# Attention beside a mixture of experts on one core: unread products, a table of slot places with gathers, and sums copied within HBM

## The reference, cut to what matters

```python
xn = _layernorm(x, axis=-1)
x = x + _L0_attn_ref(xn, ...) + _L0_ffn_ref(xn, ...)

# attention, 64 pairs of sequence and head, 1024 x 1024 scores each
attn_weights = einsum('btd,bsd->bts', q, k) + _rel_to_abs(einsum('btd,md->btm', q, rel_k[0]))
attn_probs = softmax(attn_weights)
attn_output = einsum('bts,bsd->btd', attn_probs, v) + einsum('btm,md->btd', _abs_to_rel(attn_probs), rel_v[0])
return out @ Wo + bo

# experts
top_w, top_idx = top_k(softmax(x @ gate_w + gate_b), 2)       # weights normalised over the two
h = silu(einsum('td,edf->tef', x, w1)) * einsum('td,edf->tef', x, w3)     # 256 -> 1024
out = einsum('ted,te->td', einsum('tef,efd->ted', h, w2), combine)        # 1024 -> 256
```

## Time and profile before

| | |
|---|---|
| timed runs | 1829.11, 1821.48, 1824.39 us |
| median | 1824.39 us |
| the profiled execution | 1838.71 us |
| its span, first to last instruction | 1837.0 us |
| mean granted TensorE clock | 0.945 |
| busy: PE, PEld | 1694.4 (92%), 1022.4 (56%) |
| busy: DVE, ACT, POOL | 1437.7 (78%), 1099.4 (60%), 826.2 (45%) |
| DMA | 342.69 MB, mean 187 GB/s |
| L1193, VectorE's maxima | 512 of 1.22 us |
| L1506, accumulating scatters | 78 of 1.80 us |
| L1748, VectorE's weight splits | 304, mean 1.03 us |

### The profile page before, as it was taken

The page is one execution under the profiler, slowest core; times in us unless marked ns, Lnnn a source line. Parts: engine busy times, 40 slices in busy tenths (PEclk is TensorE's granted clock), DMA queues, the critical chain, the costliest instruction groups (busy, mean ns, idle before and its releaser), DMA issues. The chain is left out here.

```text
span 1837.0 us, 35484 instructions
## 1 busy us (share of the span) xinstructions
PE 1694.4 (92%) x13756; PEld 1022.4 (56%) x13756; DVE 1437.7 (78%) x2540; ACT 1099.4 (60%) x2133; POOL 826.2 (45%) x595
## 2 busy tenths in 40 slices
PE   5998799999999999999998999999999999999991
PEld 3774223333333333333334778888788888788880
DVE  3556979998887788878675998999989999987652
...
GB/s 166 349 334 278 62 18 147 164 100 150 169 160 159 154 166 161 139 156 145 36 118 145 225 227 237 239 245 248 222 238 230 250 245 237 220 211 193 210 121 189
DMA packets 195752, 342.69 MB, mean 187 GB/s; under 512 B 33392, under 2 KB 145920, under 8 KB 187392
## 3 DMA queue, kind: packets, MB, share of 16 engines
...
...
## 5 line engine op out<-in xcount | busy, mean ns | idle before, releaser
L1193 DVE CUSTOM_DVE_ANT_0 w2s<-t_s,hide 128x1024 bf16<-128x1024 f32 x512 | 607.2, 1221 | 129.6 <-PE t_s L1048 110.0
L1328 ACT ACTIVATE t_pr<-t_s 128x512 f32<-128x512 f32 x1024 | 559.4, 604 | 186.7 <-PE t_s L1062 132.8
L1048 PE MATMUL t_s<-ks,qs 48*128 48x512 f16 x1024 | 373.4, 419 | 41.6 <-DVE t_mx L1193 25.5
L1677 ACT ACTIVATE e_sg<-e_pa,down 128x256 f32<-128x256 f32 x312 | 147.7, 473 | 399.6 <-PE e_pa L1568 395.5
L1058 PE MATMUL t_s<-qs,ks 50*128 50x512 f16 x1024 | 366.0, 402 | 10.4 <-ACT t_pr L1328 7.9
L1075 PE MATMUL t_po<-t_pr,t_vx 128*32 128x256 f32 x4096 | 348.6, 413 | 0.5 <-issue 0.3
L1577 PE MATMUL e_py<-w2s,e_hT 128*128 128x256 f32 x1248 | 323.2, 382 | 0.0
L1748 DVE SCALAR_TENSOR_TENSOR ks<-big,up,qs 128x512 f16<-128x512 f32 x304 | 310.5, 1032 | 13.5
L1506 POOL DMA_INDIRECT expert_sums<-e_y,e_token x78 | 140.5, 1801 | 293.1 <-DMA expert_sums<-e_y,e_token 203.7
L1568 PE MATMUL e_pa<-xh,qs 128*128 128x256 f16 x1248 | 240.3, 274 | 20.7 <-DVE xl L1740 17.9
L1568 PE MATMUL e_pa<-xl,qs 128*128 128x256 f16 x1248 | 239.7, 274 | 0.0
...
## 6 DMA issues: line engine op xcount, KB each, us to landing
...
```

The source lines that it names most:

```text
L1048: last = nc.tensor.matmul(s1[:, buf, half * CH:(half + 1) * CH], qs[lows, u, h, i * P:(i + 1) * P], ks[lows, u, h, half * CH:(half + 1) * ...
L1193: nc.vector.tensor_tensor_reduce(out=seen[:, buf, :], in0=s1[:, buf, :], in1=c["hide"][:, (TB - 1 - row) * P:(TB - 1 - row) * P + L], scal ...
L1328: nc.scalar.activation(pr[:, k % BP, n % HG], s2[:, turn(u, n)], ACT.Exp, scale=SPREAD ** -2).then_inc(exp_ok, 1)
```

## The change

1. **Unread products.** `idle_turns(count)` on TensorE multiplies two constants (128 x 128 by 128 x 512, 16 bits) into PSUM buffers of pass 2, which nobody reads. 18 stand ahead of the first `pass1`, 3 behind every full tile up to `rows_first` (18 tiles), 28 at the place where VectorE chooses experts, and 3 after each of 3 further tiles.
2. **First maximum rows.** For the first half of the first group the four DMAs of the second part are issued by ScalarE instead of SyncE.
3. **A table of slot places.** `slot_rows` (1040 bytes per place) becomes `slot_table` with 16 bytes, the `meta` of the row. It is filled by two DMAs of 128 x 39 runs of 16 bytes each (the spare row numbers of 128 x 2 rows behind T) behind `step(0, ...)`, beside a store of 256 rows of zeros to the normed rows. `send` scatters only `meta` (the same 64 indirect scatters, of 128 x 16 bytes); the eight loads of 512 KB in `load_rows` go.
4. **The table comes back.** SyncE, at the place where it loaded the rows of slot 0, reads the table in two parts (8 and 31 slots: 2048 and 7936 runs of 16 bytes) into SBUF. GpSimd casts each part to row numbers; after the first it issues four indirect gathers of 128 normed rows each (slots 0 and 1). After the second it writes `ones`.
5. **Gathers in the expert stage.** The rows of slot s + 1 come by two gathers of GpSimd at the head of its slot s, ahead of `xb` and `prod`. The gates of all slots are computed once (`gates`, in slot 0); `rows_of` goes.
6. **Sums.** The two scatters of `put` no longer wait for each other, only for those of the slot before. The attention result of a tile is added to `expert_sums` by a third accumulating scatter (`add_rows`), which waits until the two have landed; `put` of the next slot waits for it. `res` keeps two tiles.
7. **The end.** `combine` goes. SyncE copies the sums to the output from HBM to HBM, 8 DMAs of 512 KB, inside the expert stage's block.

```diff
-        xn=dram("xn_rows", [T, E], F32),
+        xn=dram("xn_rows", [T + ST * P, E], F32),
-        xs=dram("slot_rows", [NS * TS, XE], F32),
-        moe=dram("expert_sums", [T + P, E], F32),
+        slots=dram("slot_table", [NS * TS, 4], F32),
+        moe=dram("expert_sums", [T + ST * P, E], F32),
...
+def gather_rows(nc, dr, xr, token, came, s, u):
+    for i in range(ST):
+        nc.gpsimd.indirect_dma_start(
+            out=xr[:, u, i, 0:E], out_offset=None, in_=dr["xn"],
+            in_offset=bass.IndirectOffsetOnAxis(ap=token[:, s * ST + i:s * ST + i + 1], axis=0)).then_inc(came[u], 16)
...
# attention, SyncE
+                            if half == 0 and j == 1:
+                                continue
                 step(0, 0, 2, 0)
                 sp.wait_ge(zero_ok, 2)
-                for z in range(N_ZERO // 2):
-                    sp.dma_start(zeros[z], zero[:].broadcast_to([P, 6, XE])).then_inc(zero_out, 16)
+                for i in range(ST):
+                    sp.dma_start(zeros[i], zero[:, i:i + 1, E:XE].broadcast_to([P, NS, XE - E])).then_inc(zero_out, 16)
+                sp.dma_start(dr["xn"][T:T + ST * P].rearrange("(i p) e -> p i e", p=P), zero[:, :, 0:E]).then_inc(zero_out, 16)
...
                 load_split(0, 1)
-                for u in range(2):
-                    sp.wait_ge(sent[u], 16 * NT)
-                sp.dma_start(xr[:, 0], slot_rows[0]).then_inc(x_in[0], 16)
+                sp.wait_ge(sent, 32 * NT)
+                slots_v = dr["slots"].rearrange("(n p) f -> p n f", p=P)
+                for i, part in enumerate((slice(0, CHUNK), slice(CHUNK, NS * ST))):
+                    sp.dma_start(tab[:, part], slots_v[:, part]).then_inc(tab_in[i], 16)
                 load_second(0)
-                sp.dma_start(xr[:, 1], slot_rows[1]).then_inc(x_in[1], 16)
                 load_second(1)
...
# attention, GpSimd
                     for k in range(2):
                         nc.gpsimd.indirect_dma_start(
-                            out=dr["xs"], out_offset=bass.IndirectOffsetOnAxis(ap=dst[:, t, k:k + 1], axis=0),
-                            in_=xn[:, m % 2, t % CT, :], in_offset=None).then_inc(sent[m % 2], 16)
+                            out=dr["slots"], out_offset=bass.IndirectOffsetOnAxis(ap=dst[:, t, k:k + 1], axis=0),
+                            in_=meta[:, t, :], in_offset=None).then_inc(sent, 16)
...
-                for u in range(2):
-                    pool.wait_ge(sent[u], 16 * NT)
+                for i, part in enumerate((slice(0, CHUNK), slice(CHUNK, NS * ST))):
+                    pool.wait_ge(tab_in[i], 16)
+                    nc.gpsimd.tensor_copy(token[:, part], tab[:, part, 0]).then_inc(token_ok, 1)
+                    pool.wait_ge(token_ok, i + 1)
+                    if i == 0:
+                        for n in range(2):
+                            gather_rows(nc, dr, xr, token, x_in, n, n)
                 nc.gpsimd.memset(ones[:], 1.0).then_inc(ones_ok, 1)
...
# attention, TensorE
+                def idle_turns(count):
+                    for r in range(count):
+                        nc.tensor.matmul(s2[:, r % B2, :], c["eye"][:, 0, :], c["hide"][:, 0:CH], start=True, stop=True)
                 done = AHEAD
+                routed = XS // 2 + 4 * B1
+                idle_turns(18)
                 for at in range(XS // 2 + 2 * B1):
                     pass1(at)
+                    if at % 2 == 1:
+                        idle_turns(3)
                 rows_first()
                 for at in range(XS // 2 + 2 * B1, AHEAD):
+                    if at == routed:
+                        idle_turns(28)
                     pass1(at)
+                    if at % 2 == 1 and at > routed:
+                        idle_turns(3)
...
# experts, GpSimd
                 def put(s, u, k):
-                    pool.wait_ge(gate_ok, s + 1)
                     pool.wait_ge(y_ok, s + 1)
                     if not isinstance(s, int) or s > 0:
                         pool.wait_ge(y_out[1 - u], 32 * (k + u))
+                    after(pool, r_out, 16 * min(s, NT))
                     for i in range(ST):
-                        if i > 0:
-                            pool.wait_ge(y_out[u], 32 * k + 16 * i)
...
+                def add_rows(t, u, k):
+                    pool.wait_ge(res_ok, t + 1)
+                    pool.wait_ge(y_out[u], 32 * (k + 1))
+                    nc.gpsimd.indirect_dma_start(
+                        out=dr["moe"], out_offset=bass.IndirectOffsetOnAxis(ap=rows_at[:, t:t + 1], axis=0),
+                        in_=res[:, u, :], in_offset=None, compute_op=ALU.add).then_inc(r_out, 16)
...
                 def slot(s, u, k, tiles=True):
+                    if 0 < s < NS - 1:
+                        pool.wait_ge(xt_ps, s)
+                        gather_rows(nc, dr, xr, token, x_in, s + 1, 1 - u)
                     if tiles:
                         pool.wait_ge(e_ok, s + 1)
                         products(s, u, k)
                     if not isinstance(s, int) or s > 0:
                         put(s - 1, 1 - u, k if u else k - 1)
+                        if s <= NT:
+                            add_rows(s - 1, 1 - u, k if u else k - 1)
...
# experts, SyncE
-                    sp.dma_start(xr[:, u], xs[s]).then_inc(x_in[u], 16)
...
+                for n in range(NC):
+                    sp.dma_start(out_v[n], sums_v[n]).then_inc(o_out, 16)
+                sp.wait_ge(o_out, 16 * NC)
...
# experts, VectorE
-                def rows_of(s, u, k):
...
+                def gates():
...
-                        if f == 2:
-                            rows_of(s, u, k)
+                        if f == 2 and first:
+                            gates()
...
-def combine(nc, dr, res, out):
```

132 lines of the change are left out of this document (53 added, 79 removed).

## The result

The changed kernel took 1798.8 us (median, 1797.8 to 1802.0), the kernel before 1822.9 (1817.4 to 1829.1): a ratio of 0.988, 95% interval 0.984 to 0.992. The forecast was 1794. The profiled execution took 1799.8 us, 38.9 less than that of before; the medians are 24.1 apart, because the profiled execution of before was itself 15.8 us above its median.

What follows compares the result with a forecast made beforehand. TensorE was taken as busy almost throughout, at two clock speeds, VectorE also near its limit in the expert stage. 1838.7 + 1 - 18 + 7 - 11 - 14.5 = 1803.2, with 9 carried over: 1794 us; 8-in-10 range 1762 to 1825.

Steps and rivals of the forecast that it cites:

- Unread products: Start of attention: 109 extra products, 6.5 us for the first 18, net 3.5 gained or 5.5 lost; 1 lost taken.
- the clock would fall again inside the first group: First attention group: even odds that the granted clock falls again despite the unread products, leaving nothing gained there.
- The table's zeros: Start of attention: two DMAs of 4992 16-byte runs replace six of 780 KB in SyncE's queue; no cost counted.
- 307 runs per us taken as a rate: Table read-back before the last group: one reading of a small-run row, giving 26 us; 5 us was taken instead.
- The stalls of the batches: Middle stage, behind scatter batches: up to 35.6 us goes if moved rows cause the stalls, otherwise nothing; 18 taken.
- My undisturbed group: Middle stage: a group without a batch takes 45.1 us, against 48.3 each for the eleven groups behind.
- The wait for `ones`: Last attention group: TensorE 6 us late behind the table's read-back, 1 more for lower clock; 7 lost, ends 2 and 28.
- the number of issues and not of runs sets the price: Table read-back before the last group: price taken near the low end, 5 us, between 0.5 and 26.
- The slots: Expert stage: 0.73 us of gates and TensorE's 0.55 us wait go; slot 20.75 us instead of 21.09, 11 gained.
- GpSimd's cycle: Expert slots: next to be late, 20.2 to 22.4 us; as the bound (chance 0.11), 1841 us at 22.4.
- The end: After the last product: eight HBM-to-HBM copies take 16 us plus 3 for issue and landing; 14.5 gained, ends 4 and 20.
- The carry-over to the median: Whole kernel: timed runs are 14.3 us shorter than the profiled one; 9 carried over, part being stalls already taken out.

Runs made afterwards that it cites:

- second pair: The kernel before and the changed kernel, both unedited, profiled again on one chip at another time: spans 1815.5 and 1804.7 us, ratio of the times 0.989.
- b_narrow: The kernel before with each attention-stage scatter moving only 16 bytes per row to an unread table, loads and zero fill kept: 0.994 of before, middle stage 538.2 us.

## Why the forecast was right, and where it was not

The time lies inside the range and 5 us from the forecast, for partly wrong reasons. Step by step:

- **Unread products** (forecast +1, 3.5 gained to 5.5 lost). Right. With the long fill the third copy came 150.7 us after the block with them and 147.0 without (two kernels that also differ elsewhere, but not ahead of that copy); with the short fill, 157.5 and 156.9. By the second copy, which no fill disturbs, it was 103.6 against 100.8, and 106.1 against 100.4. So they cost some 1 to 6 us, with single traces of one code up to 8 apart there. That the clock would fall again inside the first group was the deciding doubt, and it did.
- **"The table's zeros ... no wait of TensorE on a load shows in either place"** (forecast 0). This step failed. The sentence itself is true, and no load is waited for in the trace after either; what failed is the conclusion that the fill then costs nothing. It lengthened the distance from the second to the third copy from 46.2 us to 51.4 in this pair, and by 2.5 to 10 over all traces, without any wait on a load: TensorE idles beside it with no event to end it. The row that I used for small runs in the next part (307 runs per us taken as a rate) would have given 33 us for the 9984 runs, near the 29 that SyncE took; I had refused it there and not tried it here. Even so it wouldn't have given the loss, since nothing stood in the queue behind them.
- **The stalls of the batches** (forecast -18, 0 to 35.6). The middle value held on the second pair (-17.9) and was half of the first (-40.3), and the agreement is luck. I took all that the eleven groups lose against 45.1 us as stalls behind batches, and halved it for want of a ground. My undisturbed group was too long: without scatters a settled group takes 43.85, so the earlier trace rows hold 48 us (531.7 - 483.5) and not 36. And only a part of that is idle time without an event, 18.3 us on VectorE; TensorE's busy time is 29 us longer (502.6, 473.6) at the lower granted clock (0.95, 1.00), a term that the sum doesn't have. In the second pair, where no such stall is seen, 15 of the 18 us are VectorE's operations held up beside GpSimd's, which the sum doesn't have either. That narrow rows end the stalls isn't shown: with rows of 1040 bytes they are in one profile of before and not in the other, with rows of 16 bytes they are absent on several chips and there on the slow one.
- **The wait for `ones`** (forecast 7, 6 of them TensorE's wait). Right: 6.3, with the table landing in two steps of 8.1 and 7.2 us. Taking it out gave 8.4. That the number of issues and not of runs sets the price isn't borne out: the part of 7936 runs took 6.8 us to issue behind the first, which took 0.5, and of the fill's two equal DMAs the second took 11.0 and the first 0.4.
- **The slots** (forecast -11). This step failed too: "is 0.73 us inside that stretch and goes, so the wait of 0.55 goes too". The gates did stand in the stretch without a gap behind VectorE's last wait, but the work behind them could not come forward by as much: the `sg` for f = 3 wasn't there yet, a wait of 0.26 us opened, and a slot gained 0.1. GpSimd's cycle was forecast rightly as the next in line (20.2 to 22.4): in the changed kernel it waits for ScalarE in 8 of 30 slots, in the kernel before in all 31, and its product, begun late, held VectorE's split for 4.6 to 5.3 us in the five late slots. They went when the gathers moved under GpSimd's wait for the landing (`totals` moved in the same run).
- **The end** (forecast -14.5). Right: the copies took 16 us as taken; the 3 us for issue and landing weren't needed.
- **The carry-over to the median** (9 of 14.3 us carried over; the other 5.3 taken for stalls that go with the change). This was mis-sized. The profiled execution of before was 15.8 us above its median, and its middle stage 20 us longer than in the second profile (531.7, 511.7); that of the changed kernel was 1.0 above its own. So nearly all of the surplus went, 14.8 us. On the medians the gain was 24.1 against 30.4.

Two misses of 11 us each, the start of attention (unread products and fill, some 5 to 6 us each) and the slots, were set off in the profiled pair by the middle stage (22 us more) and the end (4 more); between the medians the middle stage gave no such surplus, and the gain fell 6 us short.

**Left open:** what stops VectorE, TensorE and ScalarE for 2 to 4 us without an event on the slow chip and in the first profile of before, most often beside a batch of scatters, and whether it hangs on the chip or its moment. A kernel without scatters, and one with spaced scatters, ran only where no such stall is seen. Narrow rows ran there and kept them. And what share of the time saved in the middle stage the change has earned at all: three kernels on the slow chip with the same code there took as long as `b_narrow` (535 to 544, 538.2).
